# Token norms of images 2 to 31: four TensorE tile products replaced by a transposing sum on VectorE, with 32x32 root tiles

## What is computed

```python
nrm = jnp.sqrt(jnp.sum(x * x, axis=-1, keepdims=True))      # x: tokens of the normalised image
nf = x / jnp.maximum(nrm, L2_EPS)
A = jnp.einsum('bnc,cd,bmd->bnm', nf, adj_w, nf)
A = softmax(5.0 * (A - jnp.max(A, axis=-1, keepdims=True)), axis=-1)
h = jnp.einsum('bmc,dc->bmd', x, affine_w) + affine_b
h = jnp.einsum('bnm,bmc->bnc', A, h)
mu = jnp.mean(h, axis=-1, keepdims=True)
var = jnp.mean(jnp.square(h - mu), axis=-1, keepdims=True)
h = (h - mu) / jnp.sqrt(var + LN_EPS) * ln_g + ln_b
h = jnp.where(h >= 0, h, NEG_SLOPE * h)
```

## Time and profile before

| what | value |
|---|---|
| median of 3 runs | 1119.42 us (1118.21 to 1122.18) |
| span of the profiled execution, which is also its own time | 1118.2 us (mean granted TensorE clock 0.986) |
| busy share of the span: TensorE, VectorE, ScalarE, GpSimd | 93%, 72%, 82%, 48% |
| chain that ended last: share of TensorE | 84% |

### The profile page before, as it was taken

How to read it: one execution, slowest core, us unless ns; L and a number is a source line. 1 busy time by engine, 2 the same in 40 slices (tenths; PEclk the granted TensorE clock), 3 DMA queues, 4 the chain that set the end, 5 groups by cost and what they waited for, 6 DMA issues and landing times.

```text
span 1118.2 us, 19802 instructions
## 1 busy us (share of the span) xinstructions
PE 1034.9 (93%) x7144; PEld 784.9 (70%) x7144; DVE 804.3 (72%) x1385; ACT 911.4 (82%) x1703; POOL 536.2 (48%) x267
## 2 busy tenths in 40 slices
PE   1199999968999999999999999999999999999994
PEld 0055555546887877777777777777777788777772
DVE  7723555578777777777777777777777777777776
ACT  1699999538888888888888888888888888888784
POOL 0044455503355555555555555555555555555543
PEclk9999999969999999999999999999999999999998
DMA  8989999730122222222322222223222222222213
GB/s 358 397 330 403 411 404 406 312 151 19 57 77 77 77 76 77 76 76 76 105 104 96 101 107 96 95 80 100 86 77 77 76 76 76 77 77 77 76 57 115
DMA packets 33421, 159.13 MB, mean 142 GB/s; under 512 B 4268, under 2 KB 4904, under 8 KB 23080
## 3 DMA queue, kind: packets, MB, share of 16 engines
q1 hardware_dynamic: 33320, 157.82, 37.1%
HBM read 136.97 MB, written 20.83 MB: 141 GB/s over the span
## 4 chain that ended last, share of the span: by engine, by line
PE 84%; DMA 7%; DVE 4%; ACT 1%; issue 1%; POOL 1%; SPq 1%; POOLq 0%; ACTq 0%; DVEq 0%
PE PS L1207 22%; PE PS L1208 21%; PE PS L1209 21%; PE PS L1225 5%; DMA Wt<-acc 4%; PE PS L1184 4%; PE PS L1174 4%; PE PS L1219 2%; PE PS L1195 2%; DMA X<-x 2%; DVE st L751 2%; PE PS L1213 2%; DMA NU<-factor_rows 0%; SPq L294 0%; PE PS L1240 0%
## 5 line engine op out<-in xcount | busy, mean ns | idle before, releaser
L928 DVE TENSOR_TENSOR Pl<-PS,Ph 128x512 fp32r<-128x512 f32 x512 | 348.1, 690 | 183.6 <-ACT PS L603 178.7
L602 ACT ACTIVATE Ph<-PS 128x512 fp32r<-128x512 f32 x384 | 235.0, 612 | 94.8 <-PE PS L1209 92.1
L603 ACT ACTIVATE PS<-PS 128x512 f32<-128x512 f32 x512 | 305.7, 611 | 7.9 <-PE PS L1209 7.9
L1207 PE MATMUL PS<-Ph,hh 128*128 128x512 f32 x512 | 206.4, 403 | 0.3 <-DVE Pl L928 0.3
L1208 PE MATMUL PS<-Pl,hh 128*128 128x512 f32 x512 | 200.0, 391 | 0.0
L1207 PE MATMUL PS<-uTh,nTh 128*128 128x512 f32 x512 | 199.9, 390 | 0.0
L1209 PE MATMUL PS<-uTh,nTl 128*128 128x512 f32 x512 | 199.6, 390 | 0.0
L1208 PE MATMUL PS<-uTl,nTh 128*128 128x512 f32 x512 | 199.6, 390 | 0.0
L1209 PE MATMUL PS<-Ph,hl 128*128 128x512 f32 x512 | 199.5, 390 | 0.0
L425 POOL TENSOR_TENSOR hl<-X,hh 128x1024 fp32r<-128x1024 f32 (+1 forms) x33 | 77.2, 2339 | 195.4 <-ACT hh L587 169.1
L408 POOL TENSOR_TENSOR LL<-LL 128x512 f32<-128x512 f32 x64 | 82.6, 1290 | 137.5 <-ACT LL L500 137.5
(11 more groups left out here) (136 smaller groups left out, 1595.5 us busy)
## 6 DMA issues: line engine op xcount, KB each, us to landing
Wt<-acc SPq DMA_DIRECT2D x64, 1024.0 KB, 7.5
out<-X SPq DMA_DIRECT2D x38, 512.0 KB, 2.6
X<-x SPq DMA_DIRECT2D x16, 1024.0 KB, 19.7
SQ<-norm_rows SPq DMA_DIRECT2D x31, 512.0 KB, 3.7
X<-factor_rows SPq DMA_DIRECT2D x31, 512.0 KB, 4.1
NU<-factor_rows SPq DMA_DIRECT2D x31, 512.0 KB, 5.0
X<-out SPq DMA_DIRECT2D x7, 512.0 KB, 5.8
out<-X SPq DMA_DIRECT2D x2, 256.0 KB, 2.4
```

The costliest lines, as they stand in the source:

```text
L602: act.activation(Ph[:, g % RING, :], sl, ACT.Exp, scale=SHARP)
L603: act.activation(sl, sl, ACT.Exp, scale=SHARP).then_inc(weights_ready, 1)
L928: dve.tensor_tensor(Pl[:, r, :], SL[r], Ph[:, r, :].bitcast(F32), ALU.subtract)\
L1207: pe.matmul(out_, lh, rh, start=start, stop=False)
```

## The change

The norms of images 0 and 1 stay as they are. For images 2 on, TensorE's `norms` go. VectorE sums the squares over each group of 32 channels with one `tensor_reduce` that transposes 32x32 blocks (`norm_sums`, at k = 2), copies the three upper groups onto partitions 0 to 31, adds the four and clamps (`norm_total`, k = 3). The sums now stand once, on a 32x32 tile. ScalarE's two root instructions work on that tile and move from k = 8 to k = 6; VectorE's Newton step works on it too, followed by a 32x32 transpose (`norm_rows_out`, k = 8). `put_rn` stores 32 rows of 32 numbers in place of 4 rows of 256. In image 0 these jobs stand at k = 6, 7, 8 and 9. In `CAST`, tile 3 gives way to tile 1. `tokens` waits for the transposing sum in place of the tile products; `queries(b, 0)` waits for `hf_ready` in place of the clamp. Nothing changes in GpSimd's list.

```diff
-CAST = (3, 7, 11, 14)
+CAST = (1, 7, 11, 14)
+KB = NPOS // 32
+SUMMED = 2
...
+        n_sums = n2x[:, 0:4 * KB].rearrange("p (g k) -> p g k", g=4)
+        n_sum, n_half, n_root, n_row = [n2a[0:32, i * KB:(i + 1) * KB] for i in range(4)]
...
             def put_rn(b):
...
+                    sp.dma_start(norm_rows[b, :].rearrange("(k i) -> k i", i=32), n_row).then_inc(n2_kept, 16)
...
             def norm_roots(b):
                 act.wait_ge(n2_clamped, b + 1)
+                if b >= SUMMED:
+                    act.activation(n_half, n_sum, ACT.Ln).then_inc(n2_roots, 1)
+                    act.wait_ge(n2_roots, 2 * b + 1)
+                    act.activation(n_root, n_half, ACT.Exp, scale=-0.5).then_inc(n2_roots, 1)
+                    return
...
-                        if k == 8 and b + 2 < B:
+                        if k == (6 if b else 8) and b + 2 < B:
                             norm_roots(b + 2)
...
+            def norm_sums(b):
+                dve.wait_ge(sq_ready, b + 1)
+                dve.tensor_reduce(n_sums[:, 0, :], ZT[b % 2].rearrange("p (k i) -> p k i", i=32), AX.X, ALU.add,
+                                  apply_transpose=True).then_inc(n2_folds, 1)
+
+            def norm_total(b):
+                at = 5 * (b - SUMMED)
+                dve.wait_ge(n2_folds, at + 1)
+
+                for g in (1, 2, 3):
+                    dve.tensor_copy(n_sums[0:32, g], n_sums[32 * g:32 * g + 32, 0]).then_inc(n2_folds, 1)
+                dve.wait_ge(n2_folds, at + 4)
+                dve.tensor_reduce(n_half, n_sums[0:32].rearrange("p g k -> p k g"), AX.X, ALU.add).then_inc(n2_folds, 1)
+                dve.wait_ge(n2_folds, at + 5)
+                dve.tensor_scalar(n_sum, n_half, NORM_MIN**2, None, ALU.max).then_inc(n2_clamped, 1)
...
+                        if k == (2 if b else 6) and b + 2 < B:
+                            norm_sums(b + 2)
+                        if k == (3 if b else 7) and b + 2 < B:
+                            norm_total(b + 2)
...
-                        if k == 7 and b + 2 < B:
-                            clamp(b + 2)
...
-                        if k == 8 and b + 2 < B:
-                            inverse_norms(b + 2)
+                        if k == (8 if b else 9) and b + 2 < B:
+                            norm_rows_out(b + 2)
...
-                        if k == 7 and b + 2 < B:
-                            norms(b + 2)
```

More of the change, by code:

```diff
@@ L185, in build @@
         n2_made = sem("n2_made")
+        n2_folds = sem("n2_folds")
         n2_clamped = sem("n2_clamped")
@@ L230, in build, with n2_before @@
         block = ctx.enter_context(nc.Block())
+        def n2_before(b):
+            return 3 * min(b, SUMMED) + 4 * max(b - SUMMED, 0)
         def sums_of(i):
@@ L305, in put_rn @@
             def put_rn(b):
-                sp.wait_ge(n2_steps, 3 * (b + 1))
-                sp.dma_start(norm_rows[b, :].rearrange("(q n) -> q n", q=Q), n2y[0:P:32, :]).then_inc(n2_kept, 16)
+                sp.wait_ge(n2_steps, n2_before(b + 1))
+                if b < SUMMED:
+                    sp.dma_start(norm_rows[b, :].rearrange("(q n) -> q n", q=Q), n2y[0:P:32, :]).then_inc(n2_kept, 16)
+                else:
+                    sp.dma_start(norm_rows[b, :].rearrange("(k i) -> k i", i=32), n_row).then_inc(n2_kept, 16)
             def load_rn(b):
@@ L563, in norm_roots @@
                 act.wait_ge(n2_clamped, b + 1)
+                if b >= SUMMED:
[3 more added lines that the diff above has]
+                    return
                 act.activation(n2a[:, :], n2x[:, :], ACT.Ln).then_inc(n2_roots, 1)
                 act.wait_ge(n2_roots, 2 * b + 1)
-                if b == 1:
+                if b:
                     act.wait_ge(first_spread, 2)
-                elif b:
-                    act.wait_ge(n2_kept, 16 * (b - 1))
                 act.activation(n2y[:, :], n2a[:, :], ACT.Exp, scale=-0.5).then_inc(n2_roots, 1)
@@ L878, in first_statistics, with norm_rows_out @@
                 last_pieces(B - AWAY + 4, B).then_inc(away_read, 1)
+            def norm_sums(b):
[11 more added lines that the diff above has]
+                dve.tensor_scalar(n_sum, n_half, NORM_MIN**2, None, ALU.max).then_inc(n2_clamped, 1)
+            def norm_rows_out(b):
+                at = n2_before(b)
+                dve.wait_ge(n2_roots, 2 * b + 2)
+                dve.scalar_tensor_tensor(out=n_half, in0=n_sum, scalar=-0.5, in1=n_root, op0=ALU.mult,
+                                         op1=ALU.mult).then_inc(n2_steps, 1)
+                dve.wait_ge(n2_steps, at + 1)
+                dve.tensor_tensor(n_half, n_half, n_root, ALU.mult).then_inc(n2_steps, 1)
+                dve.wait_ge(n2_steps, at + 2)
+                dve.scalar_tensor_tensor(out=n_root, in0=n_half, scalar=1.5, in1=n_root, op0=ALU.add,
+                                         op1=ALU.mult).then_inc(n2_steps, 1)
+                dve.wait_ge(n2_steps, at + 3)
+                if b > SUMMED:
+                    dve.wait_ge(n2_kept, 16 * (b - 1))
+                dve.transpose(n_row, n_root).then_inc(n2_steps, 1)
             def tokens(b):
-                dve.wait_ge(n2_made, b + 1)
+                if b < SUMMED:
+                    dve.wait_ge(n2_made, b + 1)
+                else:
+                    dve.wait_ge(n2_folds, 5 * (b - SUMMED) + 1)
                 dve.tensor_scalar(ZT[b % 2], X[:, place(b), :], RS[:, b:b + 1], NB[:, b:b + 1], ALU.mult, ALU.add)\
@@ L1230, in norms @@
                 pe.wait_ge(sq_ready, b + 1)
-                if b >= 2:
-                    pe.wait_ge(hf_ready, 2 * b)
                 norms_into(norms_of(b), ZT[b % 2]).then_inc(n2_made, 1)
@@ L1251, in queries @@
                     pe.wait_ge(nTl_ready, b + 1)
[L1252 to L1255, removed]
+                    pe.wait_ge(hf_ready, 2 * (b + 1))
                 h = half(e)
```

## The result

| | before | changed |
|---|---|---|
| median time | 1120.82 us (1117.95 to 1124.5, 20 runs) | 1124.15 us (1120.22 to 1128.64, 20 runs) |
| ratio, 95% interval | | 1.0030 (1.0018 to 1.0042) |
| span of the profiled execution | 1118.2 us | 1125.8 us |

The changed kernel is slower by 0.3%, just what this measurement can tell from no change. The forecast was 1.9%.

The account below looks back on a forecast made before the run. TensorE was taken as the bound, busy 26.67 of 26.67 us per image. 1118.2 - 13.8 (TensorE's gain) + 35.0 (new waits) = 1139.4 us, expected median 1140.6, 1.9% slower; range 1103.5 to 1146.

Parts of the forecast that it names:

- TensorE gains 0.44 us per image: Between tiles 7 and 8: dropping the norms saves TensorE 0.44 us in images 1 to 29, 12.8 us in all.
- The hold: Ahead of `values_full`: running GpSimd instructions hold copies and clamp, so the moments wait 1.25 us per image; chance 0.55.
- The choice between the two ends for copies: Beside GpSimd, copies are either not held or held until its instruction is over; the prediction took held.
- The wait does not move away: At k = 7: GpSimd follows TensorE's pace after the moments, so the 1.25 us wait returns in images 2 to 29.
- the term of 35.0 us: TensorE's added waits for `values_full` before the moments: 28 x 1.25 us.
- the ring: An image's length: from the moments to the end of `tokens_lower`, then 2.74 us to the next moments.
- the forecast's 27.48: Length of one image as forecast: 26.67 - 0.44 + 1.25 us.
- Image 0, -1.0 us: In image 0 the norms' wait of 2.66 us goes, but VectorE is late next: a gain of 1.0 us.
- The move of the cast costs nothing: Cast from tile 3 to tile 1: VectorE waits 1.25 us before tile 2 anyway, so no cost.
- The norm row came in time: At `queries`: the row was expected in time with 2.9 us of cover; rival of a late row, about 1134, chance 0.04.
- the first: Rival at the copies and clamp: GpSimd does not hold them, nothing waits, 1105.6 us; chance 0.33.
- The second: Rival at the copies and clamp: only the clamp is held, wait near 0.5 us, about 1119.5 us; chance 0.08.

Follow-up runs that it names:

- experiment 1: Changed kernel with `norm_total` moved from behind tile 3 to behind tile 5 in images 1 on: 1106.83 us, ratio to before 0.9888.
- experiment 6: Changed kernel with image 0 as before (image 2's norms on TensorE, old casts) and `norm_total` behind tile 5 in images 1 on: 1105.15 us, ratio to before 0.9868.
- experiment 2: Changed kernel with the three copies made into one-element `tensor_reduce` sums in the same place: 1107.07 us, ratio to before 0.9887.
- Experiment 9: Changed kernel with ScalarE's roots back at k = 8 and, from image 4 on, unused ScalarE and VectorE work added there: 1134.31 us, ratio to before 1.0136.
- Experiment 3: Changed kernel with VectorE's cast back on tile 3 instead of tile 1: 1126.97 us, ratio to before 1.0071.
- experiment 7: Kernel before with one edit, the cast moved from tile 3 to tile 1: 1120.37 us, ratio to before 1.0007.
- experiment 8: Changed kernel with ScalarE's two root instructions back from k = 6 to k = 8: 1124.91 us, ratio to before 1.0039.
- Experiment 4: Changed kernel with image 2's norms, made during image 0, put back on the tile products (`SUMMED = 3`): 1123.78 us, ratio to before 1.0043.

## Why the prediction was half right

- **TensorE gains 0.44 us per image**: right. Experiments 1 and 6 show 26.20 us, 0.47 less than 26.67. The reason given for 0.44 in place of the row's 0.64 is only in part right: the row overlaps the moments, which start 0.46 us after the norms do (580.03 and 580.49 in image 12).
- **The hold**: right, in its place and its course. One copy gets through where L458 ends, the next stands until L435 ends; from there the last copy, the small sum and the clamp take 0.86 us (forecast 0.85), and `values_full` ends 1.73 later (1.83). The choice between the two ends for copies, taken from the rate of L883 and the held L812, is borne out by experiments 1 and 2 with both values: 171 and 906 ns.
- **"The wait does not move away: GpSimd's L442 starts from `inverse_deviations` at k = 10, which follows tile 10, and thus TensorE's pace after the moments"**: this step failed. The wait returns in each of the 28 images as forecast, but it is 0.58 us and not 1.25, so the term of 35.0 us measured 14.2 by the row of waits (16.2 by 28 x 0.58). `inverse_deviations` does not stand at a fixed distance behind tile 10: ScalarE's and VectorE's jobs at k = 8 are ahead of it. The text says of ScalarE's roots there that they "shrink from 256 to 32 columns and lie off the path", and keeps the Newton step's saving for VectorE's load. Both lie on GpSimd's path: `inverse_deviations` came 0.52 us earlier, `tokens_lower` ended 0.62 earlier, and the wait is 0.67 shorter. Experiment 9 put work of that size back and got 10.3 us of wait back. With 24.68 in the ring in place of 24.06 an image would take 27.42 us, close to the forecast's 27.48.
- **Image 0, -1.0 us**: wrong in sign. From the first norms to the side jobs at k = 7 of image 1 it took 56.37 us in place of 54.27 (54.73 less image 1's own norms, 0.46). The wait for `values_full` went as said. But the forecast followed VectorE alone, and ScalarE's roots at k = 8 queue behind the total:

```profile
262.21 0.64 ACT L620 ACTIVATE PS<-PS 128x512 f32<-128x512 f32 x1
268.47 0.23 ACT L579 ACTIVATE n2a<-n2a 32x32 f32<-32x32 f32 x1 [5.61 <-DVE n2a L911]
268.73 0.23 ACT L581 ACTIVATE n2a<-n2a 32x32 f32<-32x32 f32 x1
268.86 0.57 ACT L619 ACTIVATE Ph<-PS 128x512 fp32r<-128x512 f32 x1
```

  ScalarE stands for 5.6 us with tile 9's exponentials (268.86) behind the roots, while VectorE, busy nearly throughout, gets to the clamp at 268.26. Experiment 3 (no cast moved) shows 55.45, 1.2 of the 2.1 us; experiment 7 (the cast alone) 0.76. Together 1.9. Each is one profiled execution: experiments 1, 2, 8 and 9, with image 0 as in the changed kernel, show 55.76 to 56.13, a loss of 1.5 to 1.9.
- **"The move of the cast costs nothing"**: right per image (experiment 7), short by 0.76 us in image 0.
- **Prices**: the transposing sum 1.235 us, taken at 1.22; copies and clamp 0.17, taken at 0.19; the small sum 0.375, taken at 0.3; the Newton step's four 0.18 to 0.28, taken at 0.19. The norm row came in time: there is no wait at `queries`.
- **The rivals**: the first, without a hold, was rightly priced: experiments 1 and 2 reach 1106.83 and 1107.07 us, it said 1105.6. The second said a wait near 0.5 us and about no change; the size is what came, but by another way: it had the copies free and the clamp held, and in the trace the clamp is free (170 ns) and the copies are held. Experiment 2, where only the clamp is held, has no wait but in its last image: there `tokens_lower` ends 24.00 us behind the moments, and not 24.68 as in the forecast's rows. That a wait of this size came is luck.

## What to carry to other kernels

Before a small VectorE copy or clamp goes in ahead of something that is due, look at what GpSimd is doing at that moment: in this kernel 32x32 copies took 0.17 us or up to 2.4, and moving them two tiles later, behind the instruction that was due, made 0.3% slower into 1.1% faster.

Where a new wait closes a ring through several engines, its size is the length of the whole ring less the pace of the bound engine; so a job made shorter anywhere in the ring counts, also on an engine that is off today's critical path. And the first turn of a loop, with other neighbours, wants its own list for each engine that queues there.

## What was not expected of the hardware

- Between two GpSimd instructions that follow each other at once (L458 and L435), VectorE got exactly one copy through in 27 of 28 images, and none in the other. The one issued at 607.37 ended at 607.86, 0.03 us behind L458's end at 607.83; the next was held for the whole of L435, to 610.22. Whether a longer row of small copies would cost one GpSimd instruction each is not shown. The forecast had assumed one such passage without a row that showed it.
- A VectorE sum that reduces over 32 channels by transposing runs at the rate of a plain pass: 1.235 us for 128x1024, against 1.217 for L948.
- In experiment 4 TensorE's granted clock was 0.67 for the 5.2 us after a wait of 3.15 us, and 1.00 after one of 2.66 in the kernel before. The length of the wait alone did not decide it: in experiment 7 the clock was 1.00 after a wait of 3.17 us. What did is not shown.
